# A wait for landed rows ahead of each pair of gathers in a two-layer graph network on one Trainium2 core

## The reference

```python
# layer 0, on xn = layernorm(x)
agg = jax.ops.segment_sum(xn[src], dst, num_segments=6250)
h1 = (agg + xn) @ W1 + b1            # then batch norm, relu, W2, relu

# layer 1, on the normed output of layer 0
s0, s1 = rows of src: 64 scalars, 64 x 3 vectors
messages = (four products of s0, s1 with edge_attr_4 and 64 x 64 matrices) * msg_rad
agg = jax.ops.segment_sum(messages, dst, num_segments=6250) / 4
```

## Time and profile before

| | |
|---|---|
| median of 3 runs | 3287.35 us (3279.5 to 3292.2) |
| the profiled execution | 3315.14 us, its span 3313.5 us, mean granted clock 0.927 |
| PE busy | 2769.0 us, 84% |
| POOL busy | 1844.2 us, 56% |
| DVE, ACT busy | 1823.2 us (55%), 1410.1 us (43%) |
| gathers of stage one, L921 | 654, 650.1 us of issue, from 58.6 to 1077.4 us |
| gathers of stage two, L2644 | 750, 730.9 us of issue, from 1706.6 to 2927.5 us |
| queue of POOL's DMAs, q0 | 77376 packets, 211.49 MB, 22.3% of 16 engines' span |
| queue of SP's and ACT's DMAs, q1 | 184386 packets, 232.20 MB, 23.5% |

### The profile page before, as it was taken

The page is one execution under the profiler, slowest core; times in us unless marked ns, Lnnn a source line. Parts: engine busy times, 40 slices in busy tenths (PEclk is TensorE's granted clock), DMA queues, the critical chain, the costliest instruction groups (busy, mean ns, idle before and its releaser), DMA issues. The chain is left out here.

```text
span 3313.5 us, 54301 instructions
## 1 busy us (share of the span) xinstructions
PE 2769.0 (84%) x15515; PEld 2310.4 (70%) x15515; DVE 1823.2 (55%) x5496; ACT 1410.1 (43%) x3910; POOL 1844.2 (56%) x1958
## 2 busy tenths in 40 slices
PE   1888898899888899699957787888877778769998
PEld 1667777778777788588846555566666667659998
DVE  5742223577665566545547445466555565555555
ACT  4012222244222455346544366577645565532222
POOL 5666666666666155456666555566666566624343
PEclk9999999899998999899978899899978888879999
DMA  7244444666665377345542333334435555442222
GB/s 220 77 114 124 119 122 125 193 198 207 202 204 181 124 231 224 115 132 168 163 147 82 107 92 99 103 107 117 116 108 154 145 146 143 135 137 76 76 82 66
DMA packets 269039, 453.82 MB, mean 137 GB/s; under 512 B 74642, under 2 KB 194173, under 8 KB 267670
## 3 DMA queue, kind: packets, MB, share of 16 engines
q1 hardware_dynamic: 184386, 232.20, 23.5%
q0 software_dynamic: 77376, 211.49, 22.3%
q10 hardware_dynamic: 7006, 6.97, 0.8%
HBM read 338.67 MB, written 111.83 MB: 136 GB/s over the span
## 5 line engine op out<-in xcount | busy, mean ns | idle before, releaser
L2644 POOL DMA_INDIRECT g_got<-xm_d,idx x750 | 730.9, 975 | 502.1 <-PE ps L2233 216.2
L921 POOL DMA_INDIRECT g_got<-xn_d,idx x654 | 650.1, 994 | 385.9 <-issue 185.7
L2233 PE MATMUL ps<-g_hotw,g_got 128*128 128x96 f32 (+11 forms) x3000 | 428.4, 290 | 86.2 <-issue 63.1
L2233 PEld LDWEIGHTS ps<-g_hotw,g_got 128*128 128x128 f32 x3000 | 398.5, 200 | 130.0 <-issue 129.1
L1305 PEld LDWEIGHTS ps<-g_hot,g_got 128*128 128x128 f32 x2616 | 348.1, 203 | 80.1 <-issue 71.3
L1305 PE MATMUL ps<-g_hot,g_got 128*128 128x120 f32 (+4 forms) x2616 | 360.2, 286 | 46.0 <-issue 29.6
L2702 ACT ACTIVATE g_hotw<-g_hot,g_wr 128x16 f32<-128x16 f32 (+8 forms) x1308 | 299.2, 309 | 52.9 <-DVE g_hot L632 40.1
L3011 PE MATMUL ps<-g_half 128*125 128x512 f32 x400 | 205.1, 660 | 77.0 <-ACT g_half L2673 50.2
L1112 DVE TENSOR_TENSOR g_ring<-g_ring,ps 128x40 f32 (+8 forms) x327 | 68.8, 210 | 334.6 <-remote 168.9
L2852 DVE TENSOR_TENSOR g_ring<-g_ring,ps 128x140 f32 (+9 forms) x375 | 129.8, 346 | 146.8 <-DMA p_xin<-in_x 47.9
L1440 PE MATMUL ps<-g_hT,g_w 128*128 128x250 f32 x800 | 199.9, 394 | 10.8 <-issue 8.6
(11 more groups left out here) (427 smaller groups left out, 5454.3 us busy)
## 6 DMA issues: line engine op xcount, KB each, us to landing
h_d<-gin_hid SPq DMA_DIRECT2D x23, 1000.0 KB
gin_hid<-h_d SPq DMA_DIRECT2D x23, 1000.0 KB
job_in<-jobs_d SPq DMA_DIRECT2D x54, 258.0 KB
g_got<-xm_d,idx POOLq DMA_INDIRECT x750
p_z<-z_d SPq DMA_DIRECT2D x49, 224.0 KB
g_got<-xn_d,idx POOLq DMA_INDIRECT x654
q_d<-g_qo SPq DMA_DIRECT2D x25, 250.0 KB
g_wqkv<-q_d SPq DMA_DIRECT2D x25, 250.0 KB
```

What stands on the lines that cost most here:

```text
L921: landed.start(e.indirect_dma_start(got[:, k % (2 * GB), :], None, xn_d[0:N, :], bass.IndirectOffsetOnAxis(ap=idx[:, HT + k:HT + k + 1], a ...
L2233: mm = e.matmul(to, rows[j][:, c * P:(c + 1) * P], hotw[:, j, c * w:4 * w].unsqueeze(1).broadcast_to([P, r, n]), start=(j == 0), stop=(j = ...
L2644: landed.start(e.indirect_dma_start(got[:, 2 * (n % GB) + j, :], None, xm_d[0:N, :], bass.IndirectOffsetOnAxis(ap=idx[:, at:at + 1], axis= ...
```

## The change

In both stages POOL waits, before a pair of gathers, also until the two gathers of the pair two before have landed. For the first two pairs the awaited value is zero and no wait is made.

```diff
                     def gather(k):
                         if k % 2 == 0:
                             summed.wait(e, k // 2 - GB, "sums")
+                            landed.wait(e, (k // 2 - 2) % GB, (k // 2 - 2) // GB)
                             e.sem_inc(s_held["Pool"], 1)
...
                     def gather(n):
                         summed.wait(e, n - GB, "sums")
+                        landed.wait(e, (n - 2) % GB, (n - 2) // GB)
                         e.sem_inc(s_held["Pool"], 1)
```

## The result

The changed kernel takes 3377.93 us (median of 3 runs, 3374.03 to 3387.4) where the kernel before takes 3287.35 us. The ratio is 1.0265, with a 95% interval of 1.0233 to 1.0297: 90.6 us slower. The forecast was 3290 us, in a range up to 3314. It was wrong, in the direction of the rival *slower, stage one's end starves*.

The account below looks back on a forecast made before the run. TensorE was taken to set the pace, with POOL having room. Terms: 0 in stage one, 1 us at stage two's start, 2 us at stage one's thin end; +3 us on 3287 gives 3290 us, range 3275 to 3314.

Parts of the forecast that it names:

- slower, stage one's end starves: Rival, 558 to 1094 us: added waiting exceeds POOL's room, ring drains, last sums wait; 22 us slower, 3309 us; chance 0.24.
- POOL's 101 us over: Second half of stage one: POOL's 167 pairs need 419 us of 520, leaving 101 us to absorb new waiting.
- L + h: Issue end to last packet (L), then to next pair's start (h); free to 2.81 us; quiet 2.6, busy 5.6.
- The rule weighed: Skill's fixed DMA cost, counted against the change: quiet waits would block 0.35 us a pair, giving 3297 instead of 3290.
- 0.35 x 167 = 58 pairs by 1.4 = 81 us of new waiting on POOL: Second half of stage one: busy pairs' added waiting, said to fit within 101 us with 20 us left.
- the share of 0.35: Share of busy pairs, 558 to 1090 us: 14 of 40 slices have DMA engines at seven tenths or more.
- its case of 122 us: Slower rival's case with all 167 second-half pairs busy: 234 us of waiting, 122 after the cushion, 3409 us.
- The slices speak against that: Prediction's ground, from DMA busy slices, for rejecting that all 167 pairs of stage one's second half are busy.
- Faster: Rival: fewer POOL packets under way return a quarter of TensorE's unnamed idle time, 23 us, 3264 us; chance 0.13.
- The wait does nothing: Rival: L stays under 1.6 us even in busy slices, so no wait blocks; 3287 us; chance 0.15.
- The cushion of some 27 us: Middle of stage one's second half: time rows lie in the ring before their sums; 11 us at the end.
- Stage two was costed at 1 us: Start of stage two: pair 2 may start up to 5 us later; 1 us, otherwise nothing with 283 us over.

Follow-up runs that it names:

- e4: The changed kernel with both stages waiting for the gathers six pairs back instead of two; ratio 0.9989 to the kernel before.
- e6: The changed kernel with both stages waiting for the pair just before instead of two back; ratio 1.4359 to the kernel before, 1430 us slower.
- e1: The changed kernel with the added wait kept in the gathers of stage one alone; ratio 1.0227 to the kernel before.
- e2: The changed kernel with the added wait kept in the gathers of stage two alone; ratio 1.0040 to the kernel before.
- e9: The kernel before, no landing wait, with the buffer ring emptied at eight pairs and refilled freely; ratio 1.0432 to the kernel before.

## Why the prediction was wrong

**What held.** TensorE's and POOL's rates, the 2.51 us of a pair and POOL's 101 us over stand. The wait itself is free (54301 instructions before and after, e4). L + h of a quiet pair is 2.57 us in e6 for the 2.6 that I took, so the quiet pairs are free: in pairs 14 to 159 of stage one POOL's stops before a pair, over the 0.30 us of each, sum to 72 us in the changed trace and to 73 before. The parts held too. In e6's first half the last packet of a pair ends 1.46 us after its issue (L was taken as 1.4), the last landing count comes 0.33 us later, and the next pair starts 0.78 us after that: h is 1.1 us where I took 1.2. In 43 of the 59 blocked starts named below the 0.78 is the same. The rule weighed, the fixed 2.0 us and the bytes (the Trainium skill, DMA: Bandwidth & Descriptors, Anatomy of one DMA), gave an estimate of 2.3 us if all of it lay behind the issue. Measured in e6 from the end of the issue to the last landing count are 1.8, between rule and row, and by either the quiet wait is far from costing what was lost.

**The step that failed** is the number of busy pairs, "0.35 x 167 = 58 pairs by 1.4 = 81 us of new waiting on POOL". The waiting measured in the second half of stage one is 166 us. At first sight the number looks right, for 59 pairs start blocked there; but they wait 2.81 us each. The forecast's 1.4 was the mean of two pairs: with L + h of 5.6 one start is blocked for 5.6 - 2.81 = 2.79 us, and the one behind it is free. So 58 busy pairs by 1.4 are 29 blocked starts by 2.79. The wait of a blocked start came out as forecast, and there were twice as many. They do alternate: of the 59, some six stand right behind another.

What was wrong is the share of 0.35, read from slices of 13 us in which the DMA engines were busy seven tenths or more. A landing blocks when L + h is over 2.81 us, that is, when the last landing count comes more than 2.81 - 0.78 = 2.03 us after the issue. By that measure 121 of the 167 pairs of the second half are late in the trace of before and 97 in the changed one, a share of 0.72 and 0.58. These counts were in the trace of before and I did not read them. The forecast's own 1.4 us by 121 pairs are 169 us, by 97 they are 136; the cut at 101 us over is passed by either. An estimate that replays POOL's waits pair by pair gives 173 us with the counts of before, and 151 with those of the changed trace, too little since counts are missing. The price did little harm: the mean L + h of the late pairs, by the recorded counts, is 5.2 us before and 5.5 after the change, where the forecast had 5.6, although single landings spread widely (38% of the last counts of before come over 4.4 us after the issue, the longest 9.4).

**The account with the right number.** With 166 us and 15 us of longer issues POOL has 181 us to place in 101. Before, its stops and longer issues were 90 + 11 = 101; the difference is 80 us, and the gathers of the second half take 81 us more (599 us instead of 518). None of POOL's 59 stops there is one for room in the ring: in all but 1 us of their time the sums of pair n-12 had been done for over 5 us. So in the second half it is the landings that hold POOL, and POOL that sets the end of the stage, 84 us later in the last gather (81 here, and some 3 from the first half); the cushion at the end shrinks from 16.4 to 6.4 us (last gather's start to last sums' start), which gives back 10; 74 us remain. The standstills of TensorE (30 us of idle time in the two stretches above) lie beside POOL's refills at full rate, where POOL waits for no sums, and this account needs nothing from them. Whether bursts would have fallen otherwise without them is not shown.

**The rivals.** *Slower, stage one's end starves* has the right place from pair 160 on, the right mechanism and the right point of decision: beyond 101 us of waiting and the cushion each us is one of TensorE, and 181 - 101 - 10 = 70 is near the 74 measured. Its price, 22 us, had half of the pairs busy, still too few; its case of 122 us had all of them, too many. "The slices speak against that" rested on the reading that failed. *Faster* is out: the idle time that names no instruction grew, from 30 us before the matmuls of stage one's sums to the 53 of the page, and shrank by 3 us only in stage two, from 63 to 60. *The wait does nothing* is out by e1 and e2. The argument against the slower rival, that part of L shrinks as the issue moves later, is borne out in part: the median of the last landing counts in the second half falls from 3.5 to 2.6 us behind the issue, but those over 4.4 us only from 63 pairs to 55, and what is left was enough.

**The smaller terms.** The cushion of some 27 us was there (mean 25 us from landing to sums in the second half before) and did not help, since it is a stock: 80 us of lost rate spend it three times over; it fell to a mean of 10 us, with a least value of 0.04. Stage two was costed at 1 us and is worth 13 (e2): its bursts are rarer (4% of the last counts of before come over 4.4 us after the issue, against 38% in the second half of stage one), and that the 283 us over take the rest is argued.

## What to carry over

A wait on a landing cost nothing here in the quiet pairs and all of its 91 us in the bursts. Count the late landings transfer by transfer, from their landing counts in the stretch where other queues store megabytes; the share of time in which the DMA engines are nearly full gave half the number. A mean over blocked and free pairs is no price for a blocked one. Compare the sum of these waits with what the issuing engine has over in that same stretch; a buffer ring is a stock and pays only once. If such a limit is wanted, put it where it is slack by one more period: two pairs back cost 91 us here, three back 15, six back none. On the quick chip, where POOL has no time over, the limit with a ring of 7 cost 309 us.

## What was not expected

- Chips differ: the same kernel before takes 2907.59 us on one and 3271.05 to 3301.97 on the others. On the quick one TensorE has few standstills (14 us of "issue" before stage one's sums with the ring of 7), and POOL's gathers leave 0.13 us a pair over; a ring of 7 instead of 12 is 0.7% slower there and 1.0% faster on another. So it is no version to recommend on these runs.
- On the usual chips a long series of gathers at 1.26 us each goes with a standstill of TensorE, DVE and ACT that names no cause. In e9's eight refills, of 13 to 15 pairs, TensorE is idle for 16 to 27 us each, up to 32 us at a stretch, and goes on 1 to 8 us after POOL's last issue. In one, a matmul's count was recorded 32 us after the matmul started. The cause is open.
- From the last count of a landing to the start of the next gather that waits for it are 0.78 us, the same in 43 starts.
